# Second attention: score tiles of a head in the order 512, 384, 256, 128 instead of 128, 256, 384, 512

## The reference

```
qkv = jnp.einsum('bsd,od->bso', x, w_qkv) + b_qkv
q, k, v = jnp.split(qkv, 3, axis=-1)                    # 32 heads of 16
scores = jnp.einsum('bqhd,bkhd->bhqk', q, k) * scale
scores = scores + alibi[None, :, None, :]               # slope of the head times position
scores = jnp.where(causal[None, None, :, :], scores, jnp.float32(-1000000000.0))
attn = jax.nn.softmax(scores, axis=-1)
out = jnp.einsum('bhqk,bkhd->bqhd', attn, v).reshape(B, S, D)
return jnp.einsum('bsd,od->bso', out, w_out) + b_out
```

## Time and profile before

| what | value |
|---|---|
| time, median of 3 runs | 1580.31 us (1579.23 to 1580.67) |
| the profiled execution: its time, its span | 1577.87 us, 1576.0 us |
| PE busy in the whole span | 1457.7 us (92%) |
| DVE, ACT busy in the whole span | 1020.9 us (65%), 857.8 us (54%) |
| stretch in which scores of the second attention are made | about 1095 to 1420 us |

### The profile page before, as it was taken

The page is one execution under the profiler, slowest core; times in us unless marked ns, Lnnn a source line. Parts: engine busy times, 40 slices in busy tenths (PEclk is TensorE's granted clock), DMA queues, the critical chain, the costliest instruction groups (busy, mean ns, idle before and its releaser), DMA issues. The chain is left out here.

```text
span 1576.0 us, 25393 instructions
## 1 busy us (share of the span) xinstructions
PE 1457.7 (92%) x7696; PEld 1205.1 (76%) x7696; DVE 1020.9 (65%) x2547; ACT 857.8 (54%) x2183; POOL 536.7 (34%) x467
## 2 busy tenths in 40 slices
PE   6899999999999999999887999998789899986798
PEld 4788888888888888888766888886677777764586
DVE  7767667676676766667645333354788888897643
ACT  2766555665556655566523323311888888894210
POOL 5563555545555455553310000023332214010600
PEclk9999999999999999999988999999999999997999
DMA  4010010101101000000002111106433434322000
GB/s 163 14 48 15 27 35 20 40 13 27 33 20 40 13 29 31 27 7 7 15 7 88 61 60 60 54 0 107 94 74 87 73 81 85 73 34 96 21 21 27
DMA packets 37517, 71.98 MB, mean 46 GB/s; under 512 B 4992, under 2 KB 5376, under 8 KB 36864
## 3 DMA queue, kind: packets, MB, share of 16 engines
q1 hardware_dynamic: 29664, 55.35, 11.4%
q0 software_dynamic: 7776, 15.73, 6.3%
HBM read 60.58 MB, written 10.49 MB: 45 GB/s over the span
## 5 line engine op out<-in xcount | busy, mean ns | idle before, releaser
L804 ACT ACTIVATE a_probs<-a_probs,a_least 128x512 f32<-128x512 f32 (+3 forms) x256 | 143.0, 559 | 179.6 <-DVE a_least L684 170.9
L411 POOL TENSOR_TENSOR a_rotated<-a_by_cos,a_by_sin 128x512 f32<-128x512 f32 x80 | 103.5, 1293 | 244.3 <-DVE a_by_sin L707 242.2
L692 DVE TENSOR_TENSOR a_probsT_lo<-a_ps_turn,a_probsT_hi 128x512 fp32r<-128x512 f32 (+3 forms) x256 | 118.7, 484 | 72.1 <-ACT a_probsT_hi L812 70.6
L812 ACT CAST a_probsT_hi<-a_ps_turn 128x512 fp32r<-128x512 f32 (+3 forms) x256 | 101.4, 426 | 100.9 <-PE a_ps_turn L562 100.8
L1702 ACT ACTIVATE a_probs<-a_probs,a_least 128x128 f32<-128x128 f32 (+3 forms) x256 | 142.2, 560 | 2.4 <-issue 1.5
L1590 DVE CUSTOM_DVE_ANT_0 a_probs<-f_ps_gate,a_causal 128x128 f32<-128x128 f32 (+3 forms) x256 | 116.9, 486 | 31.2 <-PE f_ps_gate L1447 21.2
L864 ACT ACTIVATE a_probs<-a_probs,a_inverse 128x128 f32<-128x128 f32 (+3 forms) x256 | 123.2, 553 | 8.6 <-DVE a_inverse L717 7.5
L64 PE MATMUL a_ps_out<-a_wo_hi,a_attended_hi 128*128 128x512 f32 x256 | 105.4, 412 | 17.6 <-POOL a_wo_lo L405 15.4
L684 DVE CUSTOM_DVE_ANT_0 a_probs<-a_ps_score,a_causal 128x512 f32<-128x512 f32 (+2 forms) x192 | 101.0, 551 | 29.4 <-PE a_ps_score L66 29.3
L421 POOL TENSOR_TENSOR a_query_lo<-a_rotated,a_query_hi 128x512 fp32r<-128x512 f32 x64 | 82.6, 1290 | 107.9 <-ACT a_query_hi L824 107.9
L736 DVE TENSOR_TENSOR x<-a_ps_out,x 128x512 f32<-128x512 f32 x64 | 44.3, 691 | 104.3 <-PE a_ps_out L66 104.3
(11 more groups left out here) (276 smaller groups left out, 4129.2 us busy)
## 6 DMA issues: line engine op xcount, KB each, us to landing
a_raw<-in_wq SPq DMA_DIRECT2D x36, 256.0 KB, 2.7
a_raw<-in_wo SPq DMA_DIRECT2D x36, 256.0 KB, 2.6
a_stacked_q<-a_spill_q POOLq DMA_DIRECT2D x48, 128.0 KB, 5.1
a_stacked_k<-a_spill_k POOLq DMA_DIRECT2D x24, 256.0 KB, 5.1
f_raw<-in_gate SPq DMA_DIRECT2D x14, 256.0 KB, 2.7
f_raw<-in_up SPq DMA_DIRECT2D x14, 256.0 KB, 2.9
f_raw<-in_down SPq DMA_DIRECT2D x14, 256.0 KB, 3.6
a_raw<-in_wk SPq DMA_DIRECT2D x12, 256.0 KB, 2.9
```

The lines of the kernel that those rows point to most:

```text
L411: nc.gpsimd.tensor_tensor(rotated[:], by_cos[:], by_sin[:], ALU.add).then_inc(rotation_added, 1)
L692: nc.vector.tensor_tensor(probsT[1][:, t % 2, 0:w], ps_turn[:, t % 2, 0:w], probsT[0][:, t % 2, 0:w].bitcast(F32), ALU.subtract).then_inc( ...
L804: nc.scalar.activation(tile, tile, ACT.Exp, bias=least[:, slot, i:i + 1], scale=-1.0, accum_out=total[:, slot, i:i + 1]).then_inc(exp_done, 1)
```

## The change

The functions that make, mask and exponentiate a score tile no longer take the tile's number i but its place in the order. The tile is i = 3 - place. So the tiles of a head come 512, 384, 256, 128 wide, on all three engines. Counts that were by tile number are now by place: the bank is place % 2, and the waits count places. Where a tile lies in `probs`, `least` and `total`, and everything that reads it there, is unchanged. The number of instructions, their shapes and their sums are the same.

```diff
--- before.py
+++ after.py
@@ -1437,14 +1437,15 @@
                     last = product(nc, ps_side, [x[:, t * P:(t + 1) * P] for x in attended], [x[:] for x in wo], True, True)
                 last.then_inc(side_made, 1)
 
-            def score(cu, u, i):
+            def score(cu, u, place):
+                i = QT - 1 - place
                 n, b, j = STEPS1 * cu + u, u // HPC, u % HPC
-                if i == 0 and j == 0:
+                if place == 0 and j == 0:
 
                     wait(pe, stacked_q_in, 16 * DMAS_Q * (2 * cu + b + 1))
                     wait(pe, stacked_k_in, 16 * DMAS_K * (2 * cu + b + 1))
-                wait(pe, score_masked, 4 * n + i - 1)
-                nc.tensor.matmul(ps_score[:, i % 2, 0:P * (i + 1)], stacked_q[:, b, j // 2, j % 2, i * P:(i + 1) * P],
+                wait(pe, score_masked, 4 * n + place - 1)
+                nc.tensor.matmul(ps_score[:, place % 2, 0:P * (i + 1)], stacked_q[:, b, j // 2, j % 2, i * P:(i + 1) * P],
                                  stacked_k[:, b, j // 2, 0:P * (i + 1)], start=True, stop=True).then_inc(score_made, 1)
 
             def turn(cu, u, t):
@@ -1579,16 +1580,17 @@
                 dve.wait_ge(operand_hi, operand_count(c, s))
                 nc.vector.tensor_tensor(lo[:], src[:], hi[:].bitcast(F32), ALU.subtract).then_inc(operand_split, 1)
 
-            def mask(cu, u, i):
+            def mask(cu, u, place):
+                i = QT - 1 - place
                 n = STEPS1 * cu + u
                 at, w = SCORE_AT[i], P * (i + 1)
-                if i == 0:
+                if place == 0:
                     wait(dve, turned, 3 * (n - 3))
-                dve.wait_ge(score_made, 4 * n + i + 1)
+                dve.wait_ge(score_made, 4 * n + place + 1)
 
                 dve.sem_inc(wait_passed, 1)
                 nc.vector.tensor_tensor_reduce(
-                    out=probs[:, u % 4, at:at + w], in0=ps_score[:, i % 2, 0:w], in1=causal[:, SEQ - w:SEQ],
+                    out=probs[:, u % 4, at:at + w], in0=ps_score[:, place % 2, 0:w], in1=causal[:, SEQ - w:SEQ],
                     scale=-float(HD1) ** -0.5, scalar=-LOWEST, op0=ALU.add, op1=ALU.min,
                     accum_out=least[:, u % 4, i:i + 1]).then_inc(score_masked, 1)
 
@@ -1693,12 +1695,13 @@
             norm.root(act, 0)
             norm.round(act, 0)
 
-            def exponent(cu, u, i):
+            def exponent(cu, u, place):
+                i = QT - 1 - place
                 n = STEPS1 * cu + u
                 tile = probs[:, u % 4, SCORE_AT[i]:SCORE_AT[i + 1]]
-                if i == 0 and u % 4 == 0:
+                if place == 0 and u % 4 == 0:
                     wait(act, total_inverted, 4 * cu + u // 4 - 1)
-                act.wait_ge(score_masked, 4 * n + i + 1)
+                act.wait_ge(score_masked, 4 * n + place + 1)
                 nc.scalar.activation(tile, tile, ACT.Exp, bias=least[:, u % 4, i:i + 1], scale=-1.0,
                                      accum_out=total[:, u // 4 % 2, i, u % 4:u % 4 + 1]).then_inc(exp_done, 1)
 
```

## The result

The changed kernel takes 1589.32 us as the median of 6 runs (1586.17 to 1592.85), the kernel before 1579.77 us on the same chips (6 runs). The ratio is 1.0063, with a 95% interval of 1.0046 to 1.0081: slower by 9.6 us, where the prediction had 8.4. The profiled execution took 1592.85 us with a span of 1591.0, so it lies at the slow end of the runs. Parts of the trace are therefore compared by their lengths and not by the span.

The account below looks back on a forecast made before the run. The prediction took PE's list, with short handovers to DVE and ACT, to bound the kernel. Seven periods at 1.26 us less 0.4 gave 8.4 us, so 1588.7 us, with an 8 in 10 range of 1581.0 to 1593.0.

Parts of the forecast that it names:

- What bounds the kernel: PE, DVE and ACT all near full; PE's list sets the end, with 17.6 us of its own waits in 240.
- The waits for transfers: Scores wait twice for `stacked_k`, 3.8 us in all; forecast neither to grow nor to take much back.
- The main term: PE's score 3 waits for mask 1 in the query's, keys' and values' steps: 1.26 us lost for each period.
- The values' step: Low attend comes 1.42 us after mask 0 starts, at 1289.07 from 1288.67: 0.40 us lost.
- the keys' step: PE sets the pace; mask 0 starts 0.62 us after score 0, and the attend comes 0.47 us later.
- the output steps: Four steps ahead of the query's step; DVE sets their pace, so PE is late by 0.4 us once, not four times.
- The gain at the exponentials: Spread step: turns can start 0.42 us earlier behind the narrow pair, given back at L64's wait; net 0 for six periods.
- The first period: No output product to wait for yet, so the exponentials' gain of 0.4 us is taken off once.
- No change: Rival: PE makes the delay up in the 17.6 us it waits anyway; 1581.7 to 1583.1 us, chance 0.15.
- Faster: Rival: exponentials hand over 0.42 us sooner, if mask 0 to attend stays under 1.18 us; 1576.9 us, chance 0.09.
- Clock: Rival: PE stands longer at L64 and the granted clock falls; 11 us on top, about 1600 us, chance 0.04.
- The sum: Whole kernel: 7 x 1.26 - 0.4 = 8.4 us slower, giving 1588.7 us.

Follow-up runs that it names:

- e5: All three engines take the tiles 512, 128, 384, 256 wide, where the kernel before has 128, 256, 384, 512; 1586.79 us, ratio 1.0042.
- e6: All three engines take the tiles 128, 512, 256, 384 wide, where the kernel before has 128, 256, 384, 512; 1583.78 us, ratio 1.0017.
- e1: The changed kernel with ACT's exponentials alone put back to 128, 256, 384, 512; 1593.54 us, ratio 1.0088.
- e3: The changed kernel with PE's low attend moved ahead of scores 2 and 3; 1578.01 us, ratio 0.9990.
- e2: The kernel before with ACT's exponentials alone in the order 512, 384, 256, 128; 1587.82 us, ratio 1.0054.

## Why the prediction held, and what in it didn't

**What bounds the kernel** held: PE's list sets the pace, and what is put into it counts. The prediction wanted PE's waits for masks to rise from 2.0 us to several. Those of the matmuls stayed, 2.0 and 1.6 us, as their records touch each other. Those of the weight loads rose from 4.8 to 16.6 us, and the 2.0 us for each period is the loss. Such waits are a sign and not the price, though: e5 and e6 have the same period, with 13.5 and 6.1 us of them. For the price, compare starts. The waits for transfers, 3.8 and 4.1 us, stayed as forecast.

**The main term** held in kind and size. Score 3 waits for the second mask, and the three steps with projections lose 0.34 + 0.38 + 0.35 = 1.07 us for a period, where the sum had 1.26. The values' step is 0.03 from its derivation (1.39 for 1.42). In the keys' step I was 0.09 too high. Mask 0 starts 0.67 behind score 0, where I had 0.62. The 0.10 that the second mask was to start later where DVE had waited did not come: the row after mask 0 starts 0.61 behind it, at 1289.04. And the attend came 0.23 and not 0.26 behind the read.

**The term that was mis-sized** is the output steps: "as DVE sets their pace, PE is late there by the same 0.4 once and not four times". They lose 0.37, 0.06 and 0.32 in one period, 0.75 where the sum had 0. First a fourth output step of before:

```profile
1270.92 0.48 PE L1447 MATMUL f_ps_gate<-a_stacked_k,a_stacked_q 128*128 128x128 f32 x2
1271.07 0.68 DVE L1634 TENSOR_TENSOR x<-f_ps_out,x 128x512 f32<-128x512 f32 x1
...
1271.66 0.28 DVE L1590 CUSTOM_DVE_ANT_0 a_probs<-f_ps_gate,a_causal 128x128 f32<-128x128 f32 x1
```

DVE goes from the output addition straight to mask 0, and score 0 had been made: mask 0 starts 0.74 us behind it, against 0.50 where DVE stands waiting. In a fourth output step of the changed kernel:

```profile
1362.87 0.68 DVE L1636 TENSOR_TENSOR x<-f_ps_out,x 128x512 f32<-128x512 f32 x1
...
1363.11 0.65 PE L1448 MATMUL f_ps_gate<-a_stacked_k,a_stacked_q 128*128 128x512 f32 x2
...
1363.78 0.69 DVE L1592 CUSTOM_DVE_ANT_0 a_probs<-f_ps_gate,a_causal 128x512 f32<-128x512 f32 x1 [0.23 <-PE f_ps_gate L1448]
```

DVE stands 0.23 us for score 0. With the narrow masks behind the splits, and PE late, DVE comes early, and mask 0 is set by PE: 1363.78 is again 0.67 behind score 0. So DVE no longer sets the pace. As I read these rows, a closed circle does, from score 0 to the masks to score 3 to the next step's score 0, and it takes its 0.3 to 0.4 in each step. Only the third output step, with the division on DVE, is still DVE's. I had carried DVE's pace of before over to a kernel in which it had work moved off the path.

**The gain at the exponentials** is there. In the timeline of the changed kernel, from the spread step on:

```profile
1300.41 0.93 PE L1461 MATMUL f_ps_out<-ident,a_probs 128*128 128x128 f32 x7
...
1303.55 0.52 ACT L1705 ACTIVATE a_probs<-a_probs,a_least 128x256 f32<-128x256 f32 x1
...
1304.33 0.21 ACT L1705 ACTIVATION_READ_ACCUMULATOR a_probs<-a_probs,a_least 128x1 f32 x1
...
1304.67 0.98 PE L1461 MATMUL f_ps_out<-ident,a_probs 128*128 128x128 f32 x7 [0.33 <-ACT a_probs L1705]
...
1307.68 0.60 ACT L1747 CAST a_values<-f_ps_out 128x512 fp32r<-128x512 f32 x1
...
1309.16 0.47 PE L64 MATMUL f_ps_out<-a_wo_hi,a_attended_hi 128*128 128x512 f32 x1 [0.95 <-DVE a_values L1661]
```

The turns stand 0.33 us for exponentials where they stood 0.96. The narrow pair takes 1303.55 to 1304.54, 0.99 us. It is given back as forecast, since the rounding of the values comes no earlier. But L64 waits 0.95 and not 1.32, because PE arrives later by its own score waits. From the turns of the spread step to L64 it is 1309.16 - 1300.41 = 8.75 us, against 8.58. The net is 0.17 lost where I had 0.

**The first period** was given 0.4 us of gain on its own. It is 0.8 us shorter than before, though three of its steps are longer, because of a wait that I hadn't counted. It is told below. In e1 and e3 it was 45.5 and 45.0 us, so its length isn't set by the order alone; as I read it, by how that wait falls.

**The rivals.** No change: PE didn't make it up elsewhere. Faster: the handover of the exponentials was won, but the attend came 1.4 us after mask 0, above the 1.18 from which I had it decide. Clock: the granted clock was 0.99 before and after.

**The sum.** Seven periods at 1.26 less 0.4 was 8.4 us. The trace has six at 1.99, and -1.0 at the ends: 11.0, and the medians 9.6. The total came close because two errors of opposite sign met. The cost of a period was 0.7 too low, and one period of the seven, held by POOL as I read it, lost nothing.

## What to carry to other kernels

Between two engines that pass tiles through two buffers in turn, the third producer waits for the first consumers. So what stands between the first pair and the second in the producer's list must be longer than the consumer's work on the first pair: put the short tiles first, or move independent work (here one group of matmuls of 0.58 us) between the pairs. When you reorder one engine alone, look for the engine that now asks first for the tile made last: in e2, where that tile is 512 wide, it waited 23 times for 8.8 us, and in e1, where it is 128 wide, no such wait is listed. When a step lengthens one handover, work out again who sets the pace in the neighbouring steps before you call it a one-time delay.

## What the runs showed of the hardware

A DVE instruction of 128 x 256 took 5.68 us in the kernel before and 3.88 in the changed one, against 0.42 or 0.43 us in most other places. The timeline of DVE in the kernel before:

```profile
1138.15 5.68 DVE L1612 TENSOR_TENSOR a_result<-a_summed,a_inverse 128x256 f32<-128x256 f32 x1
```

The timeline of POOL in the kernel before, at the end of that instruction:

```profile
1142.30 1.25 POOL L1356 TENSOR_TENSOR a_wq_hi<-a_raw,a_zeros 128x512 fp32r<-128x512 f32 x1
1143.63 1.34 POOL L1358 TENSOR_TENSOR a_wq_lo<-a_raw,a_wq_hi 128x512 fp32r<-128x512 f32 x1
```

The same row of DVE in the changed kernel:

```profile
1140.45 3.88 DVE L1614 TENSOR_TENSOR a_result<-a_summed,a_inverse 128x256 f32<-128x256 f32 x1
```

And POOL in the changed kernel:

```profile
1142.79 1.26 POOL L1356 TENSOR_TENSOR a_wq_hi<-a_raw,a_zeros 128x512 fp32r<-128x512 f32 x1
1144.13 1.33 POOL L1358 TENSOR_TENSOR a_wq_lo<-a_raw,a_wq_hi 128x512 fp32r<-128x512 f32 x1
```

The multiplication reads two tiles in SBUF. POOL's instructions touch each other up to a pause of 0.08 us behind L1356, and the multiplication ends 0.28 us after that pause begins (1143.83 after 1143.55), in the changed kernel as well (1144.33 after 1144.05). The traces of the nine experiments have the same: it took 4.5 to 6.4 us and ended 0.23 to 0.29 us after the start of that pause, whenever it had begun. I read it so that POOL's pause set DVE's end and absorbed what the order cost ahead of it in the first period; no experiment took POOL's work away. The Trainium skill's page "SBUF — State Buffer", section "Who interferes with whom", says that a DVE instruction with two SBUF inputs contends with a GpSimd instruction that reads SBUF, and calls the contention for the shared ports an exclusive lock. By that rule, the trace agrees, with 5.68 us where 0.43 is usual. PE, without work meanwhile, came back at a granted clock of 0.61 for 4 us.
